# Two layers' junction: the tail of layer 0 and the start of layer 1 written in one sequence on each engine

## The reference

```python
x = x + tanh(g_xattn[0]) * _L0_xattn_ref(_layernorm(x), ctx_2048, causal, padding, ...)  # 32 heads of 8, 8 key groups
x = x + tanh(g_ffn[0])   * _L0_ffn_ref(_layernorm(x), w_up, w_down)
x = x + tanh(g_xattn[1]) * _L1_xattn_ref(_layernorm(x), ctx_2048, ...)  # 16 heads of 128, 8 key groups
x = x + tanh(g_ffn[1])   * _L1_ffn_ref(_layernorm(x), Wr, Win, Wout)    # top 2 of 8 experts

# _L0_ffn_ref: twice a Hadamard transform, rounding to 8 bits by each row's largest value, a product with ternary weights
h = hbitlinear(hidden_states, w_up, 8)
h = jnp.square(jax.nn.relu(h))
return hbitlinear(h, w_down, 8)

# _L1_xattn_ref: its own rows and the context as keys, two attentions side by side
ln_out = _ln(hidden_states, ln_w, ln_b)
q = _ln(_fp8_linear_pertensor(ln_out, wq, wq_scale, q_in_scale).reshape(b, s, g, hpg, d), qln_w, qln_b)
k = _ln(_fp8_linear_pertensor(ln_out, wk, ...)); v = _fp8_linear_pertensor(ln_out, wv, ...)
core = _gqa(q, k, v)
xout = _gqa(qx, kx, vx)                  # qx from the rows, kx and vx from cond
cat = jnp.concatenate([core, xout], axis=-1)
catq = _div_clamp_fp8(cat, proj_smooth)
return jnp.einsum('bsi,oi->bso', catq, wproj) * (proj_in_scale * proj_w_scale)
```

## Time and profile before

| | |
|---|---|
| median of 3 runs | 1464.71 us (1464.11 to 1464.71) |
| profiled execution: its time, its span | 1465.79 us, 1464.1 us |
| instructions in the profile | 29786 |
| TensorE busy | 1292.1 us, 88% |
| VectorE busy | 1042.8 us, 71% |
| ScalarE busy | 920.9 us, 63% |
| GpSimd busy | 754.2 us, 52% |

### The profile page before, as it was taken

How to read it: one execution, slowest core, us unless ns; L and a number is a source line. 1 busy time by engine, 2 the same in 40 slices (tenths; PEclk the granted TensorE clock), 3 DMA queues, 4 the chain that set the end, 5 groups by cost and what they waited for, 6 DMA issues and landing times. The chain is left out here.

```text
span 1464.1 us, 29786 instructions
## 1 busy us (share of the span) xinstructions
PE 1292.1 (88%) x8832; PEld 949.8 (65%) x8847; DVE 1042.8 (71%) x2336; ACT 920.9 (63%) x3577; POOL 754.2 (52%) x1068
## 2 busy tenths in 40 slices
PE   3899999999963899999999999999999994359991
PEld 2234444444432688888888888888888883349991
DVE  6466666666544888888888888888888877835554
ACT  1245454554534988888888888888888863313230
POOL 2355464645432566666666666666655542723331
PEclk8799999999985999999999999999999996569996
DMA  6443333323002311011110111101120005422225
GB/s 128 110 78 54 71 57 65 68 54 70 15 1 79 113 37 37 0 36 36 36 36 0 36 36 36 36 0 36 38 70 1 2 1 176 138 77 80 90 73 172
DMA packets 134339, 83.50 MB, mean 57 GB/s; under 512 B 67309, under 2 KB 129774, under 8 KB 134256
## 3 DMA queue, kind: packets, MB, share of 16 engines
q1 hardware_dynamic: 125280, 72.50, 19.4%
q0 software_dynamic: 3744, 8.43, 1.6%
q10 hardware_dynamic: 5232, 1.54, 0.5%
HBM read 50.01 MB, written 34.00 MB: 57 GB/s over the span
## 5 line engine op out<-in xcount | busy, mean ns | idle before, releaser
L1358 POOL TENSOR_TENSOR head_rstd<-head_rstd,minus_half 128x4 f32<-128x4 f32 x192 | 240.8, 1254 | 15.0
L1348 ACT ACTIVATE squares<-ps 128x128 bf16<-128x128 f32 x768 | 202.1, 282 | 49.9 <-PE ps L1320 39.7
L1320 PE MATMUL ps<-l_wb,xq 128*128 128x512 f16 (+1 forms) x1024 | 211.3, 329 | 6.7 <-DVE xq L1282 4.6
L1428 POOL TENSOR_TENSOR prob<-prob,rinv 128x512 f32<-128x512 f32 x128 | 135.5, 1058 | 118.0 <-DVE rinv L1423 116.5
L1415 ACT ACTIVATE prob<-ps,nmax 128x128 f32<-128x128 f32 x512 | 182.7, 384 | 11.4 <-DVE nmax L1408 11.4
L1378 ACT ACTIVATE headsT<-ps,l_hln 128x256 f32<-128x256 f32 (+1 forms) x256 | 166.6, 678 | 25.6 <-PE ps L1371 25.6
L1348 ACT ACTIVATION_READ_ACCUMULATOR squares<-ps 128x1 f32 x768 | 163.5, 214 | 0.0
L1364 DVE TENSOR_TENSOR heads_n<-ps,head_rstd 128x512 f32<-128x512 f32 x192 | 131.5, 685 | 38.8 <-POOL head_rstd L1358 38.8
L656 DVE TENSOR_REDUCE nmax<-ps 128x4 f32<-128x512 f32 x128 | 85.1, 682 | 75.4 <-PE ps L649 75.2
L1320 PEld LDWEIGHTS ps<-l_wb,xq 128*128 (+1 forms) x1024 | 101.0, 99 | 53.6 <-DVE xq L1282 5.0
L1401 PE MATMUL ps<-headsT 128*128 128x128 f32 x1024 | 135.2, 275 | 0.3 <-issue 0.3
(11 more groups left out here) (303 smaller groups left out, 2762.6 us busy)
## 6 DMA issues: line engine op xcount, KB each, us to landing
slots<-blank_slot SPq DMA_DIRECT2D x16, 1161.0 KB, 5.6
taken<-slots SPq DMA_DIRECT2D x23, 258.0 KB, 2.8
w_out_raw<-in_wprojT SPq DMA_DIRECT2D x8, 512.0 KB, 4.4
raw<-in_winT SPq DMA_DIRECT2D x4, 1024.0 KB, 9.2
raw<-in_woutT SPq DMA_DIRECT2D x4, 1024.0 KB, 6.1
back<-picked SPq DMA_DIRECT2D x8, 512.0 KB, 7.2
q_stack<-q_parts SPq DMA_DIRECT2D x48, 64.0 KB
k_blocks<-k_parts SPq DMA_DIRECT2D x192, 16.0 KB
```

Of the source, the lines that this page charges most:

```text
L1320: last = e.matmul(out, xq[:, k, which, slot_at], weights(k, hl, c0, n), start=(k == 0 and hl == 0), stop=(k == KD - 1 and hl == 1))
L1348: last = e.activation(squares[:, 4 * n + h, :], A[n][:, h * HD1:(h + 1) * HD1], ACT.Square, scale=HD1**-0.5, accum_out=hss[:, 4 * n + h:4 ...
L1358: e.tensor_tensor(hr[:, four], hr[:, four], t["half"][:, four], ALU.pow).then_inc(g_r[n].sem, 1)
L1428: e.tensor_tensor(prob[:, kind, :, :], prob[:, kind, :, :], spread(rinv[:, kind, :], P), ALU.mult).then_inc(g_p[kind].sem, 1)
```

## The change

The two layers' pieces stand in one block now. `layer0` and `layer1_attention` no longer run their parts; each returns a `Layer` (its pieces and their order before, in and after the loop), and `joined` writes both for each engine: layer 0's counters, what stands before its loop, the loop, then **layer 1's counters**, then layer 0's last stages (a), layer 1's first pieces with `const` at their head (b) and the eight WP pieces (c), in the sequence that a string of letters for the engine gives (`MIXED`), and then layer 1's loop and what follows it. The clearing of counters stands behind layer 1 and takes both layers' in one range.

Four things follow from that in the code:

- layer 1's tiles lie at the addresses of layer 0's (`over`), and its banks are layer 0's: A:0 to A:3 use banks 0, 2, 1 and 3, the scores 5 and 4, PV and O 6 and 7. Pieces of layer 1's first item (round 0) wait with `spent` until layer 0's last use of the tile or bank is counted;
- RS waits for layer 0's F7v of the sample it reads, RA and the root step SU of the first item for `const`;
- WP's ring of raw weights has 2 places where it had 4;
- the program has only so many counters, so that several pairs and triples of them became one with two or three steps for each item, in both layers' loops (for instance `f_bn`, `f_stat`; `g_s`, `g_r`; `r_p`, `r_rstd`). In the loops the value that such a step waits for takes register instructions: on GpSimd a turn of layer 0 has 71 entries in its list instead of 62, and a turn of layer 1 55 instead of 48; on TensorE the loops are the same.

The core of the diff:

```diff
+class Layer:
...
+    def __init__(self, s, before, after, body, loop):
+        self.s, self.before, self.after, self.body, self.loop = s, before, after, body, loop
+
+    def emit(self, e, owner, steps):
+        for name, *more in steps:
+            if (name, owner) in self.s.pieces:
+                self.s.pieces[(name, owner)](e, *more)
+
+    def prime(self, e, owner):
+        for flag in self.s.flags.get(owner, []):
+            flag.prime(e)
+
+    def repeat(self, e, owner):
+        with e.Fori(*self.loop(owner)) as i:
+            self.emit(e, owner, self.body(owner, i))
+
...
+def both(owner, hook, first, second, aside, mixed):
+    @hook
+    def _(e):
+        first.prime(e, owner)
+        first.emit(e, owner, first.before(owner))
+        first.repeat(e, owner)
+        second.prime(e, owner)
+        turns = {"a": (first, list(first.after(owner))), "b": (second, list(second.before(owner))), "c": (second, list(aside(owner)))}
+        for letter in mixed[owner]:
+            layer, steps = turns[letter]
+            layer.emit(e, owner, [steps.pop(0)])
+        assert not any(steps for _, steps in turns.values())
+        second.repeat(e, owner)
+        second.emit(e, owner, second.after(owner))
...
-        e.bn_stats(st[:, :], row(i)).then_inc(first.sem, 1)
-        e.wait_ge(first.sem, first.at(i))
+    def statistics(e, i, st, m, done):
+        e.bn_stats(st[:, :], row(i)).then_inc(done.sem, 1)
+        e.wait_ge(done.sem, done.at(i, 1))
         e.memset(spare[:, :], 0.0)
...
+    final = {"pe_qkv": pe_qkv, "pe_S": pe_S, "pe_ST": pe_ST, "pe_PV": pe_PV, "pe_OB": pe_OB, "g_mask": g_mask, "g_ulow": g_ulow,
+             "v_nl": v_nl, "v_max": v_max, "a_exp": a_exp, "v_part": v_part, "v_o": v_o, "a_hT": a_hT, "v_x2": v_x2}
+    layer = Layer(s, lambda owner: starting(owner, bounds(owner)[0]), lambda owner: some(owner, bounds(owner)[1], B + B), turn,
+                  lambda owner: tuple(n // 2 for n in bounds(owner)))
+    return layer, psum, places, final, small
...
-def layer1_attention(nc, a, t, ctx):
+def layer1_attention(nc, a, t, ctx, bank, places, final, small):
     def sb(name, shape, dt=F32):
         return ctx.enter_context(nc.sbuf_tensor(name, shape, dt))
 
+
+    def over(place, name, shape, dt=F32, after=0):
+        return nc.alloc_sbuf_tensor_at(name, shape, dt, offset=places[place] + after)
+
+    def spent(e, *names):
+        for name in names:
+            e.wait_ge(final[name].sem, final[name].at(B - 1))
+
+    def first(i):
...
-    A, S, O = bank[0:4], bank[4:6], bank[6:8]
-    squares, hss, hr = sb("squares", [P, 12, HD1], BF16), sb("head_squares", [P, 12]), sb("head_rstd", [P, 12])
...
     @s.piece("RS", "vector")
     def _(e, b, i):
+        if isinstance(b, int):
+            e.wait_ge(final["v_x2"].sem, final["v_x2"].at(b if b < AHEAD else B - 1))
         e.wait_ge(r_n.sem, r_n.at(b - 1))
-        e.bn_stats(stats[:, :], x[:, bass.ds(b, 1), :].rearrange("p b d -> p (b d)")).then_inc(r_bn.sem, 1)
-        e.wait_ge(r_bn.sem, r_bn.at(b))
+        e.bn_stats(stats[:, :], x[:, bass.ds(b, 1), :].rearrange("p b d -> p (b d)")).then_inc(r_stat.sem, 1)
+        e.wait_ge(r_stat.sem, r_stat.at(b, 1))
```

```diff
-        for step in part(owner, -AHEAD, 1):
-            steps.append(step)
-            while n < len(after) and after[n] == step:
-                steps.append(("WP", n))
-                n += 1
-        assert n == len(after), (owner, after[n:])
-        return steps
-
...
+        return ([("const",)] if owner == "vector" else []) + part(owner, -AHEAD, 1)
+
+    def aside(owner):
+        return [("WP", n) for n in range(WP_EIGHTHS)] if (("WP", owner)) in s.pieces else []
+
+    return Layer(s, starting, lambda owner: part(owner, B - AHEAD, B + 1), lambda owner, b: rounds(ORDER1[owner], b, False),
+                 lambda owner: (1, B - AHEAD)), aside
...
+    "gpsimd": "aaaaaaaaaaaaaaaaaaaaaaaaaaaaaaaaaaaaaaaaaaaababaabbaaabbaabbaabbabbbbbbbbbbbbbbbbbbbbbbbbbbbbb",
+    "sync": "aaaaaaaabcccbbccccc",
...
 def program(nc, a, out, phases):
     t = common_tiles(nc)
-    low = nc.alloc_semaphore("layer0_first").num
-    with ExitStack() as both:
-        layer1_tiles(nc, t, both)
-        with ExitStack() as ctx:
-            layer0(nc, a, t, ctx)
-        spent = range(low, nc.alloc_semaphore("layer0_last").num + 1)
+    t["filled"] = nc.alloc_semaphore("slots_filled")
+    low = nc.alloc_semaphore("layers_first").num
+    with ExitStack() as ctx:
+        layer1_tiles(nc, t, ctx)
+        first, bank, places, final, small = layer0(nc, a, t, ctx)
+        second, aside = layer1_attention(nc, a, t, ctx, bank, places, final, small)
+        with nc.Block() as block:
+            joined(block, first, second, aside, MIXED)
+        spent = range(low, nc.alloc_semaphore("layers_last").num + 1)
         with nc.Block() as block:
             @block.gpsimd
             def _(e):
                 e.sem_clear(spent)
         nc.extend_free_semaphores(list(spent))
-        with ExitStack() as ctx:
-            layer1_attention(nc, a, t, ctx)
```

190 lines of the change are left out of this document (118 added, 72 removed), and 3 rows, old and new, of the table OUTPUT_AFTER.

## The result

The changed kernel takes 1431.07 us (median of 4 runs, 1430.66 to 1431.52), the kernel before on the same chip 1464.71 (1464.11 to 1465.11). The ratio is 0.9771, with a 95% interval of 0.9754 to 0.9788: faster by 33.6 us. The profiled execution took 1431.25 us with a span of 1429.2.

What follows compares the result with a forecast made beforehand. Both loops were taken as bound by TensorE, the dip between them by engines waiting in turn. −37.9 + 2.0 + 1.0 + 1.9 + 1.0 = −32.0 us gave 1432.7 us; forecast range 1426 to 1439 (0.72), eight in ten 1424 to 1444.

Steps and rivals of the forecast that it cites:

- The terms of the junction: Between the layers' loops, where one chain empties and the next fills, 414 to 487.6 us: −37.9, +2.0 and +1.0 us.
- the clock: TensorE between the loops: one fall to half clock, 3.3 us long, costing 2.0 us, from 0 to 6.
- the counters: TensorE setting layer 1's 15 semaphore counters behind layer 0's loop: costs 1.0 us, between 0 and 1.7.
- the late weights: Four of eight o-projection weight eighths split behind RT(2), where ScalarE is nearly full: costs 1.0 us, from 0 to 3.
- the clearing: Semaphore clearing of both layers, moved behind layer 1: costs 1.9 us, from 0 to 3.9.
- The walk: Durations carried through the new lists to RT of sample 2: from 487.61 to 449.7 us, gain 37.9.
- the sign that the prediction named: End of layer 0's tail: the walk is wrong if F7d(15) comes before 446 or behind 453 us.
- Station 1: VectorE, constants 3.72 us and sample 0's statistics 0.65 ahead of L813: 4.37 in 4.82 us of idle time, costing nothing.
- the rivals: Alternative outcomes: tail hardly lengthened 0.08, half clock or worse waits 0.15, loops pay 0.02, nothing overlaps 0.01, slower 0.02.
- The tail was lengthened: Rival on layer 0's tail: it grows by only 0 to 2 us, giving 1420 to 1426 us; chance 0.08.
- The loops pay nothing: Rival in both loops: shared counters' register instructions on GpSimd cost some 13 us, giving 1440 to 1450; chance 0.02.
- TensorE left the junction at full clock: Rival at layer 1's loop entry: TensorE stays at 1.2 GHz, each round costs 11.35 us more, five give 1489; chance 0.02.

Runs made afterwards that it cites:

- the counters' experiment: Kernel before with only the pairs and triples of counters merged in both layers' loops, order unchanged: 1463.39 us against 1464.22, ratio 0.9992.
- the trace with the idle matmuls: Changed kernel plus 8, 6, 13 and 19 unused identity matmuls in TensorE's waits: 1429.23 us.
- the tail-first pair: Changed kernel with layer 0's last stages ahead of layer 1's pieces on every engine: 1479.34 us; the same with the constants at their early place: 1475.65 us.
- F6 alone: Changed kernel with F6 of sample 15 moved ahead of SC:1, TQ:2 and A:1 on TensorE: 1432.38 us.
- F6 with F6q: Kernel with fewer idle matmuls and spread eighths (1430.62 us), F6(15) moved ahead on TensorE and F6q(15) on VectorE, 4 idle matmuls before F7(15): 1426.85 us.

## Why the prediction was right, and where its terms were not

**The sum.** Forecast was 1432.7, measured 1431.07. Of the rest of 1.6 the traces say this. The terms of the junction came to -34.9 (-37.9, +2.0 for the clock, +1.0 for the counters) and measured -33.5 (-33.8 from F7v(11) on, and 0.34 for the counters ahead of it); the late weights 1.0, measured 0.8; the clearing 1.9, measured 1.1. Together -32.0 forecast and -31.5 measured. The medians are 33.6 apart, 2.1 more than that. What makes up the difference is not in the sum: the trace of the changed kernel is 2.99 us ahead already at F7v(0), before anything was changed in order, and the trace of the kernel before is itself 1.1 us over its median.

**That start.** In the thirteen kernels in which it is the same program, but for merged counters and the places of tiles, F7v(0) lies between 127.68 and 130.67 us, and what differs is how long TensorE waits for the scattered rows of layer 0's first samples, by DMA. These are its first wait of that kind in the kernel before, and in the changed one:

```profile
33.04 0.61 PE L648 MATMUL ps<-mask,minus 128*128 128x512 bf16 x1 [8.22 <-DMA k_blocks<-k_parts]
```

```profile
30.82 0.61 PE L694 MATMUL ps<-mask,minus 128*128 128x512 bf16 x1 [6.60 <-DMA k_blocks<-k_parts]
```

In the kernels built on the kernel before it was 8.22, 6.58 (counters merged) and 7.68 us; in those on the changed one 5.68 to 7.14. A small part is the merged counters: VectorE sets 15 at the start instead of 17, and TensorE's first row comes at 7.89 or 7.90 us instead of 8.08. The rest I take for the spread of single executions, of which the trace before is the slowest. But the two traces without merged counters are also the two slowest of the thirteen (130.67 and 129.72, the others up to 129.52), so that the merging has a larger part in it, or the places of the tiles one, stays open; the medians of the counters' experiment are 0.8 apart, which its interval does not tell from nothing.

**Station by station.** Against F7v(11), F6q(13) was 1.2 us late (forecast 1.0), F4(14) 1.6 (1.8), F7d(13) 2.8 (2.4), F6(14) 3.5 (2.7), F3(15) 4.1 (2.9), F7d(14) 7.5 (3.8), F6(15) 7.3 (4.9), F7d(15) 10.1 (5.9). The walk was made for full clock, so it is better held against the trace with the idle matmuls, in which the clock is held up: there F7d(13) is 2.2 late, F6(14) 2.7, F3(15) 4.2, F7d(14) 5.0, F6(15) 6.5 and F7d(15) 7.6. Up to F6(14) the walk is right within 0.3 us; between F6(14) and F3(15) it misses 1.3, and that error stays, with 0.4 more at the end. What delays F3(15) by the 1.3 is not shown. By the sign that the prediction named, the walk is at its edge: F7d(15) at 450.72 us is inside the 446 to 453, but with the 2.65 us of the earlier start taken out it is at 453.4, the clock's 2.4 us included. Station 1, which priced the constants at nothing, is wrong in size: with the statistics they take 6.2 us and not 4.37 in the hole of 4.82, so the addition L813 comes 17.10 us behind F7v(11) instead of 15.81, 1.3 late. F6q(13), the next station, is 1.2 late where 1.0 was forecast, so the total was hardly touched by it, and the tail-first pair shows 3.7 us that the constants are worth.

**The term that was mis-sized: the clock.** The prediction expected "one fall of that kind", 3.3 us at half clock, and named over 10 us between 414 and 470 as the sign that the term is wrong. There were three falls and 13.6 us: 3.4 in the stretch from 415 (5.0 us at 0.66), 6.8 up to 436.8, 3.4 from 447 (4.0 us at 0.57). With the clock held up RT(2) comes 2.4 us earlier. The cost (2.0 taken, 2.4 measured at least) was near by luck: there were more falls than I expected, but most of what ran slowly had time. TensorE was busy for some 12 us of the 13.6; by an estimate from that, it lost 6 us of its own time, and 2.4 came back when the clock was held. The Trainium skill (TensorE: Matmul & The Clock Gate, What's actually happening) takes the throttled state for the default that activity lifts; the trace agrees in that the clock came back each time with work, and not in the 0 us that I derived for a junction that is never idle for long: the first fall lies around a wait of 1.42 us, the second around one of 2.18, and the third comes with the wait of 1.00 behind the one of 2.91.

**The walk itself** was up to 1.7 us too short: with full clock RT(2) is 36.2 us ahead, where the walk had 37.9 (the idle matmuls, which delay a piece here and there, are in the 36.2). The counters on TensorE were forecast at 1.0 and cost 0.34, VectorE's 1.74 us at the old change of block notwithstanding; that error covered part of the walk's. So the junction came out right within 1.4 us by three terms that were off by 1.7, 0.4 and -0.7. The clearing was put too high by 0.8, and the start's lead was in no term. The mechanism was right; that the total came within 1.6 us is in part luck.

**The late weights** were near in size, 0.8 for 1.0, from a wrong count. The prediction has four of the eight eighths split ahead of RT(2). In the kernel before ScalarE has split all eight ahead of it and VectorE six; in the changed one it is six and five. The price is the wait of 1.21 us behind the two that were left for the end, not the work of four.

**Nothing came of the rivals.** The tail was lengthened by 10 us and not by 0 to 2. The loops pay nothing: between the first five and the last three, rounds are 11.23 to 11.58 us apart in all fourteen kernels. TensorE left the junction at full clock.

**What the prediction did not price.** "Nothing else costs", it said, and the ring of two is in none of its terms. That holds only because the eighths were moved too, into layer 0's tail, where a load has time to land before the next is due: in the changed kernel's trace ScalarE waits for none of the eight. With the ring alone the kernel is 17.7 us slower. The sentence that names the cover and its price was missing.

## What to carry to other kernels

Two chains that fill and empty an engine one after the other can be laid side by side; take a landmark behind which both orders are the same, and carry durations through the lists. Ahead of that, take the cheap parts of such a junction by themselves: a change of block (3.6 us) and weights that are prepared in the middle of the second chain (5.9) gave 9.5 of 33.8 us without any interleaving, and setup work that moves into an earlier wait gave 3.7 more in a pair of its own. Loads whose ring is too short for the place at which they are used can take all of it back: 17.7 us. When one engine's piece is moved ahead, look at the list of the engine that consumes it: F6 alone gained nothing, F6 with F6q gained 0.9 us. And put a landmark ahead of everything that moved: counters set ahead of F7v(11) did not show in the distance from it.

## What was not expected of the hardware

- At waits of TensorE of 1.42, 2.18 and 2.91 us stand stretches of half clock (0.66, 0.50, 0.57 granted); filling them with unused matmuls held 1.00 and was worth 2.4 us.
- Setting layer 1's counters behind a busy loop costs TensorE 0.34 us, and at the kernel's start 2.2 us, where all engines wait for the first rows.
- Clearing both layers' counters once took 0.87 us.
- The first 130 us, nearly the same instructions in thirteen kernels, differ by up to 3 us, by the DMAs that write and read back rows.
- Small steps of VectorE on 128x3 and 128x1 took 0.58 to 0.65 us instead of 0.16 to 0.17 in a stretch where GpSimd was at work without a break; the cause is not shown.
- The same sixteen matmuls of layer 1's last o-projection took 1.92 us in one trace and 3.29 in another, behind the same wait of 3.8 us, at different granted clocks.
